# A recurrence on TensorE without the visit to its loop's code: what moves in the first ten microseconds

## The reference, cut to what matters

```python
h = silu(cond @ W1.T + b1)
gate = sigmoid(h @ W2.T + b2)
x1 = x * (2 + gate)                     # x + (v + v * gate)
prev = cond                             # h0
for t in range(256):
    prev = tanh(prev @ Wh + x1[:, t] @ Wx + b)
    out[:, t] = x1[:, t] + prev
```

## Time and profile before

| what | us |
|---|---|
| median of 3 runs | 197.54 |
| the runs | 197.27 to 198.22 |
| the profiled execution, its time | 197.27 |
| the profiled execution, its span in the trace | 195.3 |
| around the span | 1.97 |
| PE busy, of the span | 176.3 |
| from the span's start to the loop's first weight load | 9.81 |

### The profile page before, as it was taken

The page is one execution under the profiler, slowest core; times in us unless marked ns, Lnnn a source line. Parts: engine busy times, 40 slices in busy tenths (PEclk is TensorE's granted clock), DMA queues, the critical chain, the costliest instruction groups (busy, mean ns, idle before and its releaser), DMA issues.

```text
span 195.3 us, 33383 instructions
## 1 busy us (share of the span) xinstructions
PE 176.3 (90%) x15962; PEld 164.9 (84%) x15962; DVE 97.3 (50%) x395; ACT 76.8 (39%) x518; POOL 0.5 (0%) x5
## 2 busy tenths in 40 slices
PE   5799999999999999999999999999999999999995
PEld 3788898898888889889888888988988888898895
DVE  0545546545555554654555555465455555546543
ACT  3234443344433444334443344433444334443342
POOL 1000000000000000000000000000000000000000
PEclk9999999999999999999999999999999999999999
DMA  6419999402020110202002020200202020020212
GB/s 201 132 42 371 414 409 412 187 0 107 0 107 2 45 64 0 107 0 107 0 22 87 0 109 0 107 0 2 107 0 107 0 107 2 0 109 0 107 54 54
DMA packets 7105, 17.98 MB, mean 92 GB/s; under 512 B 1459, under 2 KB 2867, under 8 KB 7094
## 3 DMA queue, kind: packets, MB, share of 16 engines
q1 hardware_dynamic: 6656, 17.32, 23.6%
q10 hardware_dynamic: 438, 0.55, 0.8%
HBM read 9.48 MB, written 8.39 MB: 91 GB/s over the span
## 4 chain that ended last, share of the span: by engine, by line
PE 87%; ACT 7%; DMA 2%; issue 2%; SPq 0%
PE bank_e L193 49%; PE bank_l L193 38%; ACT h_ring L178 7%; DMA w_t<-in_w 2%; SPq L129 0%
## 5 line engine op out<-in xcount | busy, mean ns | idle before, releaser
L193 PE MATMUL bank_e<-h_ring,wh_sb 128*32 128x32 f32 x4096 | 103.1, 200 | 14.1 <-ACT h_ring L178 14.1
L193 PE MATMUL bank_l<-h_ring,wh_sb 128*32 128x32 f32 x4096 | 99.2, 196 | 0.0
L193 PEld LDWEIGHTS bank_e<-h_ring,wh_sb 128*32 128x32 f32 x4096 | 75.6, 109 | 23.8 <-ACT h_ring L178 21.1
L178 ACT ACTIVATE h_ring<-bank_e 128x32 f32<-128x32 f32 x256 | 50.6, 198 | 111.1 <-PE bank_e L193 111.1
L339 DVE TENSOR_TENSOR x<-x,h_ring 128x128 f32<-128x128 f32 x129 | 37.6, 291 | 86.3 <-ACT h_ring L178 86.3
L193 PE MATMUL bank_l<-x_ring,wx_sb 128*32 128x32 f32 (+1 forms) x4112 | 79.7, 199 | 0.0
L193 PEld LDWEIGHTS bank_l<-h_ring,wh_sb 128*32 128x32 f32 x4096 | 77.3, 111 | 0.0
L193 PE MATMUL bank_e<-x_ring,wx_sb 128*32 128x64 f32 (+1 forms) x2056 | 73.9, 227 | 0.0
L193 PEld LDWEIGHTS bank_l<-x_ring,wx_sb 128*32 128x32 f32 (+1 forms) x4112 | 61.9, 110 | 0.0
L193 PE MATMUL bank_l<-ones,b_sb 128*32 128x32 bf16 (+1 forms) x1026 | 53.9, 180 | 0.0
L178 ACT ACTIVATE h_ring<-bank_l 128x32 f32<-128x32 f32 x256 | 50.3, 197 | 0.0
(11 more groups left out here) (31 smaller groups left out, 14.1 us busy)
## 6 DMA issues: line engine op xcount, KB each, us to landing
x<-in_x SPq DMA_DIRECT2D x15, 512.0 KB, 9.3
out_dram<-x SPq DMA_DIRECT2D x15, 512.0 KB, 3.5
w_t<-in_w SPq DMA_DIRECT2D x1, 256.0 KB, 4.8
wx_sb<-in_wx SPq DMA_DIRECT2D x1, 256.0 KB, 5.1
wh_sb<-in_wh ACTq DMA_DIRECT2D x1, 256.0 KB, 4.4
x<-in_x SPq DMA_DIRECT2D x1, 256.0 KB, 3.1
out_dram<-x SPq DMA_DIRECT2D x1, 256.0 KB, 2.4
w_t<-in_w_cond ACTq DMA_DIRECT2D x1, 145.0 KB, 3.0
```

What stands on the lines that cost most here:

```text
L178: nc.scalar.activation(h_ring[:, m, s * B:(s + 1) * B], z_of(s, m), ACT.Tanh)\
L193: done = nc.tensor.matmul(out[q:q + columns], weights[:, q:q + columns], moving, start=start, stop=stop, skip_group_check=True)
```

## The change

PE's branch to `pe_visit`, the block itself and the alignment ahead of it are gone; the loop's head moves from slot 6 to slot 0 of a fetch block. The idle products are all 512 wide over the whole array: six ahead of the first gate product (three before), one between the two gate products, two behind the second. `b` is issued by SP behind `wx` and not by ACT ahead of `wh`. `one` is set ahead of `ones`, and both count on one semaphore. The first `z` is laid in another order: bias, input of k = 0, then for each half of the result `cond @ Wh` and the input of k = 1, so that half 0 is whole before half 1 is taken up.

```diff
@@ sync
             sp.dma_start(wx_sb[:], wx).then_inc(wx_loaded, DMA)
+            sp.wait_ge(b_cleared, 2)
+            sp.dma_start(b_sb[32:97:32, :, :], b_rows).then_inc(b_loaded, DMA)
@@ scalar
             act.dma_start(x_head[:], x_first).then_inc(x_head_loaded, DMA)
-            act.wait_ge(b_cleared, 2)
-            act.dma_start(b_sb[32:97:32, :, :], b_rows).then_inc(b_loaded, DMA)
             act.dma_start(wh_sb[:], wh).then_inc(wh_loaded, DMA)
-            act.wait_ge(ones_ready, 1)
+            act.wait_ge(ones_ready, 2)
@@ tensor
-            def keep_warm(n):
-                for _ in range(n):
-                    by_columns(idle_ps, ones[:], ones[:, 0:1].to_broadcast([P, 512]), start=True, stop=True, columns=64)
-            pe.wait_ge(ones_ready, 1)
-            warm_up(3)
-            nc.br("pe_visit", engines=only_pe)
-            stage = nc.switch_bb("pe_first_stage")
+            pe.wait_ge(ones_ready, 2)
+            keep_busy(6)
...
-            keep_warm(1)
+            keep_busy(1)
...
-            keep_warm(1)
+            keep_busy(2)
             pe.wait_ge(b_loaded, DMA)
-            pe.wait_ge(one_ready, 1)
             lay_whole_bias(0, 2, 0)
             lay_whole_bias(0, 1, 1)
+            pe.wait_ge(first_input_ready, 1)
+            pe.wait_ge(wx_loaded, DMA)
+            for m in range(HALVES):
+                lay_input(0, 1 if m else 2, 0, m, columns=64)
             pe.wait_ge(wh_loaded, DMA)
-            for k in range(HALVES):
-                for m in range(HALVES):
+            for m in range(HALVES):
+                for k in range(HALVES):
                     recur(0, k, m, cond_t[:, k, :], columns=64)
-            for k in range(HALVES):
-                pe.wait_ge(first_input_ready, k + 1)
-                if k == 0:
-                    pe.wait_ge(wx_loaded, DMA)
-                for m in range(HALVES):
-                    done = lay_input(0, 1 if m else 2, k, m, columns=64)
-                    if k == HALVES - 1:
-                        done.then_inc(z_whole[m], 1)
+                if m == 0:
+                    pe.wait_ge(first_input_ready, 2)
+                lay_input(0, 1 if m else 2, 1, m, columns=64).then_inc(z_whole[m], 1)
...
-            pe.addr_align(bass.FETCH_BLOCK_INSTRUCTIONS, offset=0, max_nops=0)
-            nc.br("pe_loop", engines=only_pe)
-            with nc.body("pe_visit", parent=stage.parent, valid_engines=only_pe):
-                warm_up(1, 32)
-                nc.br("pe_first_stage", engines=only_pe)
-            nc.switch_bb("pe_loop")
-            with nc.Fori(1, TURNS + 1, engines=only_pe, head_slot={pe.engine: 6}) as turn:
+            with nc.Fori(1, TURNS + 1, engines=only_pe, head_slot={pe.engine: 0}) as turn:
@@ vector
+            nc.vector.memset(one[:], 1.0).then_inc(ones_ready, 1)
             nc.vector.memset(ones[:], 1.0).then_inc(ones_ready, 1)
-            nc.vector.memset(one[:], 1.0).then_inc(one_ready, 1)
```

More of the change, by code:

```diff
@@ L97, in build @@
         ones_ready = sem("ones_ready")
-        one_ready = sem("one_ready")
         b_cleared = sem("b_cleared")
@@ L182, in _, with keep_busy @@
         def _(pe):
-            def warm_up(n, columns=512):
+            def keep_busy(n, columns=512):
                 for _ in range(n):
```

## The result

| what | before | after |
|---|---|---|
| median, us | 197.85 | 198.76 |
| the executions, us | 197.26 to 198.44 | 197.09 to 199.83 |
| profiled execution, its span | 195.3 | 195.4 |
| first weight load of the loop | 9.81 | 7.98 |
| the pause of PE in the first turn | none | 1.9 |

A forecast was written before the change was run, and what follows sets the result against it. The loop is bound by `tanh`, PE's recurrent products, `tanh`, at unchanged pace; only the first stage and loop entry move. First stage 2.15 us earlier less 0.65 stall gives 1.5: 197.27 - 1.5 = 195.8 us, range 195.0 to 197.2.

The forecast's parts named there:

- late DMA engine: First stage: the visit's instruction packet holds one DMA engine about 1 us behind; without it `w2` lands 0.96 us earlier.
- The second product, `gate`, `b_ready`: First stage: second gate product starts at 5.05 to 5.1, `gate` comes at 5.65, `b_ready` at 7.3.
- forecast 2.15: First stage: the loop's first weight load comes at 7.65 instead of 9.81, 2.15 us earlier.
- The fetch does come back at the loop: Loop entry: without the visit, PE's entry calls for the second code block, needed at its 128th load.
- Rival (1): The packet at 3.2 isn't the visit's and comes anyway; `w2` stays at 6.01, no stall: 196.1 us; chance 0.12.
- rival (3): `w2` slips, its engine late for another reason or yielding to `wh`, and the stall is full: 197.4 us; chance 0.09.
- So the block lands at T0 + 1.1 to T0 + 2.4: a stall of 0 to 1.3 us: Loop's first turn: PE stalls once for the second code block, taken as 0.65 us.
- T0: Time of the loop's first weight load: 9.81 before the change, forecast 7.65.
- I take 2.4 GHz from about 5 on: First stage: after 4 us of unbroken full-width products PE's clock is high from about 5 us, so loads go at double pace.
- rival (2): The clock doesn't rise earlier; the loop's first load gains 0.5 us, some 0.2 of stall is left: 197.0 us; chance 0.08.
- A2: Theory from the follow-ups: PE's clock rises early in all executions and falls in the first turn's pause; no chance given.

The follow-up runs named there:

- early visit: The change with the `pe_visit` branch and block put back where they were, behind `keep_busy(6)`: 197.85 us, ratio 0.9994 to the kernel before.
- second profile of the change: The changed kernel run once more with no edit: 197.90 us, ratio 1.0028 to the kernel before; the profiled execution took 197.88.
- visit later still: The change with the visit put behind the wait for `wx` and the input of k = 0: 197.51 us, ratio 0.9987 to the kernel before.
- late visit: The change with the visit put back behind `keep_busy(2)` and the second gate product: 198.20 us, ratio 0.9987 to the kernel before.
- ten products: The late visit with `keep_busy(10)`, ten wide products at the start and not six: 200.19 to 202.75 us, ratio 1.0196 to the kernel before.
- last run above: The changed kernel, no edit, one more profiled execution for its slow group: 198.86 us.
- last version: The late visit with `b` issued by ACT ahead of `wh`, twelve executions: 196.18 us against 198.15 for the kernel before, ratio 0.9933.

## Why the prediction was wrong

**Right, point by point.** The late DMA engine was the instruction packet's doing, and the visit's: `w2` takes 3.5 us without an early packet (3.3 in before without the visit), 4.8 in before and 5.2 with the early visit. That is 1.3 to 1.7 us for a packet of 0.96; why it is more than the packet's length isn't shown. The second product, `gate`, `b_ready`: all within 0.05 us in an execution with a high clock. The first stage's gain there was 1.83 of the forecast 2.15. The fetch does come back at the loop, at the 128th load. Rival (1) falls with that, and rival (3) too: `w2` didn't slip. That these times came out within 0.05 us is in part luck: the clock rose where it was assumed in a minority of the executions.

**The first step that failed: "So the block lands at T0 + 1.1 to T0 + 2.4: a stall of 0 to 1.3 us", taken as 0.65.** It measured 1.90. The landing itself was right: the packet ends at about 9.7, T0 + 1.7. I had counted the block as usable when its packet ends. It isn't: the packet of the first profile starts at 8.7 to 8.8 and lasts 0.599 x 0.1 x 16 = 0.96, so it ends at about 9.7, and PE goes on at 11.07, 1.4 later. The same sum gives 1.4 in the second profile of the change, 1.3 in the visit later still, and 1.4 at the late visit with ten products, whose packet lasts 1.65 us (103.2% of a 0.1 us window); in four more profiles, of the low clock, it is 1.3 to 1.4. With that term the range of the stall would have been 1.3 to 2.6, its middle 1.95, and the forecast 197.27 - 2.15 + 1.95 = 197.1, no change; that still lies inside the forecast's 195.0 to 197.2, so this step alone doesn't give the median of 198.76. The row that I took for the length of a fetch shows where it begins and ends on the DMA engine, and nothing in the profile of before shows when PE could use it, since there it was early by microseconds. The end to take was that of an unknown, not that of the nearest row.

**The second step that failed: "I take 2.4 GHz from about 5 on".** That is so in some executions only: by their times 3 of 16 and 6 of 10 of the change; two of these nine were profiled. In the profiled ones of the others (the last run above, and the change with `b` on ACT) the clock rises after 13 us, inside the loop, which begins at the low pace. This step is what takes the median out of the forecast. It is rival (2), to which I gave 0.08; it is the more frequent case, and dearer than its 197.0: 198.4 to 199.8. The rival was sized as if the loop could not run at the low clock, because before's profile has the rise at 9.2, just ahead of the loop, and it had the loop start 0.5 us earlier. Measured, the loop starts 0.2 later, since the wide idle products lie on PE's chain (and without them PE waits for `b` instead, as seen), and the rise comes some 4 us later than before's. Moving the first stage forward doesn't move the rise with it.

**What cancels what.** With the early rise 1.83 is gained and 1.90 paid. With the late rise nothing is gained at the loop's entry, and 2.2 us are paid in its first four steps, of which 0.4 is the pause (5.11 against the late visit's 4.69 for the same five `tanh`), though the first `tanh` is 0.46 early. The measured 0.37% is the mixture of the two.

**The crossing.** In the profiles of the change, going from the loop's first block to the second costs 1.9 and 2.1 us at the high clock and 0.6 at the low one. The Trainium skill, "Runtime: NRT & Kernel Launch", section "Instruction fetch mechanics", calls the cost of crossing a 16 KiB boundary "mostly hidden"; in this kernel it isn't. The same section has the next page fetched while the current one runs. With that the trace agrees: in the change the packet starts at 8.7, while PE runs the loop's first block from 7.98 to 9.17.

**Left open.** Why the clock rises early in one execution and late in the next of the same kernel; why the rise is so much later than before's; whether in some executions of the change it also falls in the pause (A2): the mean granted clock is 0.991 in 4 of 16, at 198.4 to 199.4 us, and none of them was profiled (the profile with ten wide products has 0.983 with a recorded low stretch of 7 us, so an estimate from it is 3.5 us at 0.991); and why `b` on ACT moved no lower group.

## What to carry to other kernels

A step that looks like idle work, such as a short visit to code that is needed later, may be there for its side effect: look for instruction packets in the DMA queues, and ask for each block of code when it is called and when it is needed. Both ends can be had in this kernel: put the visit where its packet delays no transfer that is waited for, and 3.5 to 4.2 us ahead of the block's use (in the first profile the branch to the loop stands at 7.5 and the use at 11.07); here that gives 0.67%. Check that the visited block is itself there, or the visit costs more than it saves (202.6 us with ten products). And before a stage is moved forward, ask whether what follows it will start at the high clock; one profiled execution doesn't answer that, the spread of the executions does.

## What the runs showed of the hardware

- A block of PE's code is usable 3.5 to 4.2 us after the branch that calls it (7.5 to 11.07 in the change, 7.0 to 11.17 with the visit later still): one packet on one DMA engine, mostly 0.96 us (1.65 in the worst case seen), and 1.3 to 1.4 us from the packet's end until PE issues from the block. With the packet among the first loads, `w2` takes 4.8 and 5.2 us against 3.5.
- A block that isn't there when PE branches to it costs all of it at once: the branch lasted 4.2 us and PE loaded no weights for 3.8, at the visit with ten products.
- PE seems to keep at least three blocks: the loop lies in two of them, a third is fetched when PE enters the second (I take it from the packet at 11.85 in before), and in 64 turns no further packet comes: two in the whole span.
- The time of the clock's rise differs between executions of one kernel, before the second gate product in one of the change and at 13.4 us in another, 197.2 and 198.9 us. In the last version the groups are 2.3 us apart (196.2 and 198.5), of which only the upper was profiled. With ten products it fell while PE stood idle: the products ended at 8.17, and the granted clock was 1.00 up to 10.0 and 0.54 from there to 11.5. Through the 1.9 us pause of the change the pace stayed high (steps of 0.72 us behind it).
- The loop's steps are 1.0 to 1.2 us at the low clock against 0.72, the wait of ACT between two `tanh` 0.66 to 0.87 us instead of 0.43.
